# Group-norm centring moved from a matmul into the value weights and first states, with a separate order and PSUM bank for every piece of every group

## Chip, cores and metric

One core of a Trainium2 chip runs the whole program. The metric is the device time of one execution in microseconds (us); lower is better. The time before is 1021.75 us, the median of 3 runs (1021.67 to 1021.78). About 0.2% of that (2 us) is what a measurement can tell from no change.

## What is computed

Two blocks in a row on 64 batches of 64 positions with 256 channels. L0 is a cross attention (16 heads of 16 channels, 128 keys, of which some are masked), an output projection, an rms norm, an MLP with gelu, and a residual. L1 is a recurrent block of the RWKV kind. Cut to what the change touches:

```python
xm = xa[:, :, None] + sx[:, :, None] * (maa_stack + xxx)      # five mixes, low rank xxx
w = exp(-exp(time_decay + tanh(xw @ td_w1) @ td_w2))           # decay; td_w1 is 256 x 64
r, k, v = xr @ Wr.T, xk @ Wk.T, xv @ Wv.T                      # 32 heads of 8 channels
g = silu(xg @ Wg.T)
s0 = state[:, 2:2 + 8].reshape(b, h, 8, 8)                     # the first state of each head
# per position: out_j = sum_i r_i * (u_i * k_i * v_j + s_ij);  s_ij = k_i * v_j + w_i * s_ij
og = out.reshape(b, l, h, 8)
m = og.mean(-1, keepdims=True)
va = ((og - m) ** 2).mean(-1, keepdims=True)
og = ((og - m) / sqrt(va + 1e-05)).reshape(b, l, e) * gn_w + gn_b
x1 = x + og * g @ Wo.T                                         # then a second norm and a feed-forward
```

The output is linear in v_j and in the first state s_ij over j, so the mean over a head's 8 output channels can be taken from the columns of Wv and from the first state instead of from the output.

## The kernel before

**Tiling.** Channels lie on the 128 partitions in two halves. The 64 batches go in 16 groups of 4, so a tile is 128 x 2 x 256 in fp32. Every fp32 matmul shows in the trace as two TensorE instructions (x2 in the counts).

**Pieces.** The work of a group is cut into named pieces, and each engine has a list of `group:piece` tokens that sets its order. There is no scheduler at run time: an engine runs its list and waits on semaphores. Before, a list consists of an explicit start (`PE_FIRST` and so on), one steady turn (`PE_ORDER` and so on) that is repeated for turns 4 to 14, and an explicit end (`PE_LAST`). A steady turn carries the attention of group g+1 together with the recurrent block of group g and the feed-forward of the group before, and so on; in the steady turn every group also uses the same PSUM banks (`BANK`), with exceptions for the first and last groups.

**TensorE pieces used below** (line numbers of the kernel before): `tr0` to `tr7` transposes of attention weights (L528), `sc0`/`sc1` scores (L514), `va0`/`va1` weighted values (L540), `w0` to `w3` and `c0` to `c3` the MLP (L457 and L566), `mean0`/`var0` the first norm of L1 and `mean1`/`var1` the second (all L462), `maa` the low-rank input (L584 full width, then L587 for the fifth mix on 32-column tiles), `xp` and `x4` its outputs (L596, L606), `td1`/`td2` the decay's low rank (L613, L622), `K V R G` (L457), `coef` the bonus weights (L642), `ga0`/`ga1` the sum over i of r_i s_ij on 32-column tiles (L636), `cen` the centring (L646: one 128x128 matrix times 128x512), `gvar` the variance per head (L649), `O`, `fk`, `fr`, `fv` (L457).

**The chain from var0 to xp.** TensorE `var0`; ScalarE `lnr0` (L672, L674); VectorE `nm0` (L957); ScalarE `sh0` (L771); VectorE `sx0` (L969) and `z` (L847); TensorE `maa`; ScalarE `th` (L777, L778); TensorE `xp`. VectorE `tm0` to `tm4` and GpSimd `xm0` to `xm4` (L1063) follow, and then `td1`, K, V, R, G.

**The chain of the recurrence.** ScalarE copies V (`vr`), eight DMAs spread it over partitions, VectorE forms `kv0` to `kv7` (L1002) and runs eight scans `st0` to `st7` (L1011), GpSimd multiplies each by r (`rs0` to `rs7`, L1080), TensorE gathers four at a time (`ga0`, `ga1`). VectorE `sum` (L1021) adds the bonus; TensorE `cen` subtracts the mean into PSUM; ScalarE `gsq` squares it (L818); TensorE `gvar`; ScalarE `lng` (L672, L674); VectorE `gn` (L1025); ScalarE `gu` (L825); VectorE `og` (L1029); TensorE `O`; VectorE `res` (L1033); then the second norm, `fk`, `fr`, GpSimd `act`, `fv`, `fin` and the store.

**Other things.** `WARM` lists places where TensorE runs matmuls of ones (L467) before a piece; they compute nothing that is used. ScalarE switches between two sets of function tables (L684). The first state enters `kv[..., 0]` by a ScalarE copy, `first` (L801). `bonus` shares its memory with `gt`, the gate's tanh, and `gsq`, `g_rs` with `og`.

Of the kernel before, what the change touches and what calls it, by code (L numbers as in the profile page):

```python
# [163 lines left out]

def turns(first, order, last):

    pieces = tokens(order)
# [998 lines left out]
```

## Time and profile before

| | |
|---|---|
| median of 3 runs | 1021.75 us |
| the profiled execution: span, and its own device time | 1021.2 us span; the page gives no second time, so the sum is made on the span |
| TensorE busy (matmul) | 989.1 us, 97% |
| VectorE, ScalarE, GpSimd busy | 723.5, 756.3, 483.4 us |
| steady turn | 58.86 us |
| TensorE clock | 0.997 of full speed on average |

The span lies 0.55 us under the median, so a saving on the span is taken one to one off the median. TensorE is busy nearly all the time from the first group to the last. The steady turn can be read off the chain that ended last, where the same rows come back every 58.86 us ten times, and the last 100 us are different: there TensorE waits for the other engines, and matmuls of ones stand in the gaps.

### The profile page before, as it was taken

What the parts mean: (1) busy time and instruction counts of PE and PEld (TensorE: products, weight loads), DVE (VectorE), ACT (ScalarE), POOL (GpSimd) and SP (SyncE); (2) the same over time, 40 slices, a digit from 0 to 9 for tenths busy, and PEclk for the clock granted to TensorE, in tenths of its full rate; (3) what the DMA queues carried; (4) which work ended last, traced back from release to release, by engine and by line L of the source; (5) the groups of instructions that cost most, each with busy time, mean ns of one, the idle gap of its engine ahead of it and who ended that gap; (6) DMA issues with size and microseconds to landing.
All of it is one profiled execution on the core that took longest, in us unless ns stands there. A gap on an engine that the chain in (4) does not pass through costs nothing.

```text
span 1021.2 us, 19227 instructions
## 1 busy us (share of the span) xinstructions
PE 989.1 (97%) x6914; PEld 740.5 (73%) x6914; DVE 723.5 (71%) x1275; ACT 756.3 (74%) x2034; POOL 483.4 (47%) x391
## 2 busy tenths in 40 slices
...
DMA packets 37662, 60.95 MB, mean 60 GB/s; under 512 B 10496, under 2 KB 13888, under 8 KB 37440
## 3 DMA queue, kind: packets, MB, share of 16 engines
...
q14 instruction: 38, 0.31, 0.1%
...
## 4 chain that ended last, share of the span: by engine, by line
PE 88%; ACT 5%; DVE 4%; issue 2%; POOL 1%; DMA 0%; POOLq 0%; SPq 0%; DVEq 0%; ACTq 0%
PE psum L457 37%; PE psum L566 10%; PE psum L483 6%; PE psum L490 6%; PE psum L528 5%; PE psum L462 3%; PE psum L514 3%; PE psum L540 3%; PE psum L636 3%; PE psum L596 2%; PE psum L646 2%; PE psum L584 1%; PE psum L649 1%; ACT probs L712 1%; PE psum L642 1%
## 5 line engine op out<-in xcount | busy, mean ns | idle before, releaser
L1080 POOL TENSOR_TENSOR rs<-st,rr 128x512 f32<-128x512 f32 x128 | 188.8, 1485 | 232.9 <-DVE st L1011 228.3
L1055 POOL TENSOR_TENSOR probs<-probs,rsum 128x512 f32<-128x512 f32 x128 | 145.3, 1137 | 177.8 <-DVE rsum L900 177.0
L712 ACT ACTIVATE probs<-psum,neg_max 128x128 f32<-128x128 f32 x512 | 180.6, 396 | 17.3 <-DVE neg_max L895 16.9
L684 ACT ACT_TABLE_LOAD x129 | 165.5, 1283 | 2.2
L1011 DVE TENSOR_TENSOR_SCAN st<-decay,kv 128x512 f32<-128x512 f32 x128 | 162.6, 1280 | 1.3 <-POOL rs L1080 1.1
L457 PE MATMUL psum<-xm,w_sb 128*128 128x256 f32 x512 | 122.4, 386 | 0.3
L712 ACT ACTIVATION_READ_ACCUMULATOR probs<-psum,neg_max 128x1 f32 x512 | 120.9, 236 | 0.0
L457 PE MATMUL psum<-y,w_sb 128*128 128x256 f32 x512 | 115.5, 382 | 0.4 <-ACT probs L712 0.3
L457 PEld LDWEIGHTS psum<-xm,w_sb 128*128 128x128 f32 x512 | 95.2, 191 | 27.2 <-issue 12.0
L566 PE MATMUL psum<-hid,w_sb 128*128 128x256 f32 x512 | 114.3, 380 | 0.2 <-ACT hid L741 0.2
L1063 POOL TENSOR_TENSOR xm<-tmp,xs 128x512 f32<-128x512 f32 x80 | 93.6, 1188 | 31.8 <-DVE tmp L989 29.5
L457 PEld LDWEIGHTS psum<-y,w_sb 128*128 128x128 f32 x512 | 96.1, 190 | 16.6 <-issue 3.0
L566 PEld LDWEIGHTS psum<-hid,w_sb 128*128 128x128 f32 x512 | 97.0, 190 | 14.9 <-issue 1.0
L1002 DVE TENSOR_TENSOR kv<-vb,kk 128x504 f32<-128x504 f32 x128 | 101.9, 818 | 0.0
L895 DVE TENSOR_REDUCE neg_max<-psum 128x4 f32<-128x512 f32 x128 | 83.8, 675 | 23.2 <-PE psum L518 23.1
L989 DVE SCALAR_TENSOR_TENSOR tmp<-psum,vec,sx 128x256 f32<-128x256 f32 x128 | 54.5, 477 | 41.1 <-PE psum L596 33.0
L741 ACT ACTIVATE hid<-psum,vec 128x256 f32<-128x256 f32 x128 | 52.2, 472 | 41.0 <-PE psum L566 36.9
L528 PE MATMUL psum<-mats,probs 128*128 128x128 f32 x512 | 69.5, 275 | 1.9 <-ACT r_rs L672 0.7
L528 PEld LDWEIGHTS psum<-mats,probs 128*128 128x128 f32 x512 | 58.2, 141 | 15.6 <-issue 8.2
L905 DVE COPY probs_t<-psum 128x512 f32<-128x512 f32 x64 | 42.7, 685 | 32.2 <-PE psum L528 31.1
L483 PE MATMUL psum<-h_sb,w_sb 128*128 128x512 f32 x128 | 62.9, 616 | 1.0 <-DVE tmp L989 1.0
L457 PE MATMUL psum<-xf,w_sb 128*128 128x256 f32 x256 | 60.4, 381 | 1.8 <-DVE xf L847 1.7
...
## 6 DMA issues: line engine op xcount, KB each, us to landing
vb<-vr SPq DMA_DIRECT2D x128, 256.0 KB, 7.5
...
```

The lines of the kernel that those rows point to most:

```text
L457: last = mm(to[:, n * T:(n + 1) * T], w(name, k, m * P, m * P + P), rhs[k], start=(k == 0), stop=(k == 1))
L483: last = mm(to, w("k", k, m * P, m * P + P), h_sb[:, k, :, :], start=(k == 0), stop=(k == 1))
L528: last = nc.tensor.transpose(to[:, n * P:(n + 1) * P], probs[:, u % PROBS, n, :], mat("ident"))
L566: last = mm(to[:, m * T:(m + 1) * T], w2_sb[:, 2 * n + i, m * P:(m + 1) * P], hid[:, n % 2, i, :], start=(n == 0 and i == 0 and m == 0), s ...
L684: sc.preload_act_table_set(table)
L712: last = fn(probs[:, u % PROBS, n, :], bank(g, f"s{u}")[:, n * P:(n + 1) * P], ACT.Exp, bias=neg_max[:, u % PROBS, n:n + 1], accum_out=sum ...
L895: nc.vector.tensor_reduce(neg_max[:, u % PROBS, :], bank(g, f"s{u}").rearrange("p (n k) -> p n k", n=4), AX.X, ALU.max, negate=True).then_ ...
L1002: tt(kv[:, j, :, 1:S], batches(vb[:, j, :])[:, :, 0:S - 1], batches(flat(kk))[:, :, 0:S - 1], ALU.mult).then_inc(kv_made.sem, 1)
L1011: nc.vector.tensor_tensor_scan(st[:, n % 2, :], decay[:, :, :, :].rearrange("p h b s -> p (h b s)"), kv[:, j, :, :].rearrange("p b s -> p ...
L1055: tt(probs[:, u % PROBS, :, :], probs[:, u % PROBS, :, :], rsum[:, u % PROBS, :].unsqueeze(2).broadcast_to([P, 4, KEYS]), ALU.mult).then_i ...
L1063: tt(xm[:, k % XM, :, :].rearrange("p h (b s) -> p (h b) s", b=GB), tmp[:, k % TMP, :, :].rearrange("p h (b s) -> p (h b) s", b=GB), xs[0] ...
L1080: tt(rs[:, (RH * g + n) % RS, :], st[:, n % 2, :], flat(rr), ALU.mult).then_inc(rs_made.sem, 1)
```

## The change

- **Centring.** The TensorE piece `cen` and its matrix are gone. At the start VectorE takes from each column of Wv the mean over its head (`fold2`: two reductions, four scalar_tensor_tensor). For every group the first state is centred by VectorE (`first` moves there from ScalarE: one reduction to 128x8 and one scalar_tensor_tensor of 128x64). `gsq` and `gn` read the centred sum in SBUF (`bonus`, now a tensor of its own) instead of the PSUM bank of `cen`.
- **32-column tiles.** `td1` is issued as 8 matmuls of 32 weight columns instead of 4 of 64. `maa` is split into the tokens `maaa` and `maab`, which stand next to each other everywhere.
- **Orders and banks.** All five lists are written out for all 16 groups, with no repeated turn, and `BANKS` gives each opened bank by its position. `WARM` goes from 154 matmuls of ones to 138. The lists are some 150 lines of tokens; a line or two tells nothing, so the places on which the prediction rests are shown as instruction orders below.

```diff
-FILLS, FOLDS = 3, 26
+FILLS, FOLDS = 3, 30
...
-def turns(first, order, last):
-
-    pieces = tokens(order)
-    steady = [(i - lag, piece) for i in range(FIRST_TURNS, LAST_TURN) for lag, piece in pieces
-              if 0 <= i - lag < GROUPS and (piece not in ONCE or i == lag)]
-    return tokens(first) + steady + tokens(last)
...
-            bank = GROUP_BANK.get(g, {}).get(name, BANK[name])
+            bank = int(BANKS[len(use)])
...
+        bonus = sb("bonus", [P, HALVES, T])
+        rk, gsq, g_rs = z, og, og
...
                         for i in range(2):
-                            last = mm(to[DD * i:DD * i + DD, 0:TH], w("td1", k), xm[:, (MIX * g) % XM, k, i * TH:(i + 1) * TH], start=(k == 0), stop=(k == 1))
+                            for d in range(2):
+                                at = DD * i + 32 * d
+                                last = mm(to[at:at + 32, 0:TH], w("td1", k, 32 * d, 32 * d + 32), xm[:, (MIX * g) % XM, k, i * TH:(i + 1) * TH],
+                                          start=(k == 0), stop=(k == 1))
...
-                elif piece == "cen":
-                    taken(pe, g, "red")
-                    mm(opened(g, "cen"), center[:, :], flat(bonus), start=True, stop=True).then_inc(filled_by(g, "cen"), 1)
...
-                elif piece == "first":
-                    wait(sc, st_made, g, 0)
-                    wait(sc, s0_in, g, 16)
-                    fn(kv[:, :, :, 0], s0_sb[:, :, :, :].rearrange("p j h b -> p j (h b)"), ACT.Copy).then_inc(first_made.sem, 1)
...
-                    ready(sc, g, "cen")
-                    fn(flat(gsq), bank(g, "cen"), ACT.Square).then_inc(gsq_made.sem, 1)
+                    taken(sc, g, "red")
+                    fn(flat(gsq), flat(bonus), ACT.Square).then_inc(gsq_made.sem, 1)
...
+                    for k in range(2):
+                        nc.vector.tensor_reduce(wv_mean[:, k, :, :], vb[:, k, 0:C].rearrange("p (m j h) -> p m h j", m=HALVES, j=RH), AX.X,
+                                                ALU.add).then_inc(folded.sem, 1)
...
+                elif piece == "first":
+                    wait(ve, st_made, g, 0)
+                    wait(ve, s0_in, g, 16)
+                    flat_s0 = s0_sb[:, :, :, :].rearrange("p j h b -> p j (h b)")
+                    nc.vector.tensor_reduce(s0_mean[:, :], flat_s0.rearrange("p j c -> p c j"), AX.X, ALU.add).then_inc(s0_summed.sem, 1)
+                    wait(ve, s0_summed, g, 1)
+                    stt(kv[:, :, :, 0], s0_mean[:, :].unsqueeze(1).broadcast_to([P, RH, HALVES * GB]), -1.0 / RH, flat_s0,
+                        ALU.mult, ALU.add).then_inc(first_made.sem, 1)
...
-                    wait(ve, gsq_made, g, 1)
+                    taken(ve, g, "red")
                     wait(ve, grstd_made, g, 1)
-                    tt(flat(og), bank(g, "cen"), flat(g_rs), ALU.mult).then_inc(freed_by(g, "cen"), 1)
+                    tt(flat(og), flat(bonus), flat(g_rs), ALU.mult).then_inc(gn_made.sem, 1)
```

TensorE, a steady turn before, from `var0` of one group to the scores of the next. The rows are var0, fr, ga1, fv, tr0 and tr1, maa (two), cen, xp, gvar:

```order
L462 MATMUL psum<-hsum,mats 128x256
L457 MATMUL psum<-xf,w_sb 128x256 x4
L636 MATMUL psum<-rs,heads 32x512 x4
L457 MATMUL psum<-xc,w_sb 128x256 x4
L528 MATMUL psum<-mats,probs 128x128 x8
L584 MATMUL psum<-z,w_sb 128x256 x2
L587 MATMUL psum<-z,w_sb 32x128 x4
L646 MATMUL psum<-gt,center 128x512
L596 MATMUL psum<-th,maa_sb 128x256 x8
L649 MATMUL psum<-og,same 128x512
```

The same place after, in the turn of group 5 (var0, ga1, fr, fv, maaa, maab, tr1 and tr0, xp, gvar):

```order
L514 MATMUL psum<-hsum,mats 128x256
L693 MATMUL psum<-rs,heads 32x512 x4
L509 MATMUL psum<-xf,w_sb 128x256 x4
L509 MATMUL psum<-xc,w_sb 128x256 x4
L636 MATMUL psum<-z,w_sb 128x256 x2
L641 MATMUL psum<-z,w_sb 32x128 x4
L580 MATMUL psum<-mats,probs 128x128 x8
L650 MATMUL psum<-th,maa_sb 128x256 x8
L703 MATMUL psum<-og,same 128x512
```

The two transposes that stood ahead of `maa` now stand behind it, where `cen` was.

ScalarE, near the end before: from the copy of V of group 15 (`vr`). The row `og<-psum` of L818 is `gsq` of group 14, and `rr`, `kk` are R and K of group 15:

```order
L678 ACTIVATE vr<-psum 128x512
L782 ACTIVATE tw<-psum 128x128
L684 ACT_TABLE_LOAD
L787 ACTIVATE decay<-psum,vec 128x4x63 x2
L801 ACTIVATE kv<-s_sb 128x64
L818 ACTIVATE og<-psum 128x512
L793 ACTIVATE decay<-decay 128x8x63
L678 ACTIVATE rr<-psum 128x512
L678 ACTIVATE kk<-psum 128x512
L672 ACTIVATE og<-psum,vec 128x512
```

And after, where `gsq` is L868:

```order
L868 ACTIVATE og<-bonus 128x512
L836 ACTIVATE tw<-psum 128x128
L732 ACTIVATE vr<-psum 128x512
L738 ACT_TABLE_LOAD
L726 ACTIVATE og<-psum,vec 128x512
L728 ACTIVATE og<-og 128x512
L875 ACTIVATE og<-og,gnv 128x256 x2
L732 ACTIVATE kk<-psum 128x512
L786 ACTIVATE decay<-psum,vec 128x4x63 x2
L732 ACTIVATE rr<-psum 128x512
```

The squaring of group 14 has moved from behind group 15's V, tw and e1 to ahead of them.

VectorE, the scans of group 15 before: from the first scan (`st0`), with `kv0` to `kv2` and `og` of group 14 ahead of it:

```order
L1002 TENSOR_TENSOR kv<-vb,kk 128x8x63 x3
L1029 TENSOR_TENSOR og<-og,gate 128x512
L1011 SCALAR_TENSOR_TENSOR st<-decay,kv 128x512
L1002 TENSOR_TENSOR kv<-vb,kk 128x8x63
L1033 TENSOR_TENSOR x<-psum,x 128x512
L940 TENSOR_TENSOR hsum<-x 128x256
L1011 SCALAR_TENSOR_TENSOR st<-decay,kv 128x512
```

And after:

```order
L1095 TENSOR_TENSOR og<-og,gate 128x512
L1099 TENSOR_TENSOR x<-psum,x 128x512
L998 TENSOR_TENSOR hsum<-x 128x256
L1060 TENSOR_TENSOR kv<-vb,kk 128x8x63
L1069 SCALAR_TENSOR_TENSOR st<-decay,kv 128x512
L1060 TENSOR_TENSOR kv<-vb,kk 128x8x63
L1006 TENSOR_TENSOR xc<-x,psum 128x512
L1069 SCALAR_TENSOR_TENSOR st<-decay,kv 128x512
```

`og`, `res` and `hm1` of group 14 now stand ahead of group 15's scans and no longer between them.

## Rows read from the trace of the kernel before

**Rows 1.** Windows: length, then busy us of PE, PEld, DVE, ACT, POOL; clock, DMA

```profile
334.78:393.64 58.86, 58.62 (x423) 45.38 (x423) 43.78 (x79) 46.99 (x128) 30.04 (x25) 1.00 0.33 58
...
805.78:867.71 61.93, 61.04 (x432) 46.38 (x431) 45.28 (x80) 47.73 (x135) 31.04 (x25) 1.00 0.31 52
...
972.00:1021.20 49.20, 36.94 (x162) 19.80 (x162) 23.78 (x32) 14.13 (x23) 13.68 (x10) 1.00 0.03 11
```

**Rows 2.** TensorE timeline, steady turn: start us, length us, line, output and inputs, count

```profile
347.46 0.59 PE L462 MATMUL psum<-hsum,mats 128*128 128x256 f32 x2
347.90 1.89 PE L457 MATMUL psum<-xf,w_sb 128*128 128x256 f32 x8
349.72 1.06 PE L636 MATMUL psum<-rs,heads 128*32 128x512 f32 x8
350.71 1.99 PE L457 MATMUL psum<-xc,w_sb 128*128 128x256 f32 x8
352.54 1.04 PE L528 MATMUL psum<-mats,probs 128*128 128x128 f32 x8
353.42 1.03 PE L584 MATMUL psum<-z,w_sb 128*128 128x256 f32 x4
354.38 0.63 PE L587 MATMUL psum<-z,w_sb 128*32 128x128 f32 x8
354.94 1.12 PE L646 MATMUL psum<-gt,center 128*128 128x512 f32 x2
355.99 1.15 PE L596 MATMUL psum<-th,maa_sb 32*128 32x256 f32 x16
```

**Rows 3.** TensorE timeline, same turn: two 128x512 matmuls, and the next piece

```profile
381.28 1.88 PE L483 MATMUL psum<-h_sb,w_sb 128*128 128x512 f32 x4
383.00 0.59 PE L462 MATMUL psum<-ysum,mats 128*128 128x256 f32 x2
```

**Rows 4.** TensorE timeline, same turn: td1, scores after an idle time, va1

```profile
360.29 0.66 PE L613 MATMUL psum<-xm,w_sb 128*64 128x128 f32 x8
...
361.82 1.17 PE L514 MATMUL psum<-kt,qt 32*128 32x128 f32 x32 [0.24 <-issue]
...
374.57 1.08 PE L540 MATMUL psum<-probs_t,vv 128*32 128x128 f32 x32
```

**Rows 5.** VectorE timeline, steady turn: sx0 and z of the chain to maa

```profile
350.99 1.20 DVE L969 TENSOR_TENSOR sx<-xs 128x512 f32<-128x512 f32 x1 [1.15 <-ACT xs L771]
352.22 0.88 DVE L847 SCALAR_TENSOR_TENSOR z<-sx,vec,xs 128x256 f32<-128x256 f32 x2
```

**Rows 6.** GpSimd timeline, the same moment

```profile
350.61 1.03 POOL L1055 TENSOR_TENSOR probs<-probs,rsum 128x512 f32<-128x512 f32 x1
```

**Rows 7.** TensorE timeline, group 1: its var0

```profile
113.63 0.59 PE L462 MATMUL psum<-hsum,mats 128*128 128x256 f32 x2
```

**Rows 8.** VectorE timeline, group 1: its sx0 and z

```profile
117.23 0.69 DVE L969 TENSOR_TENSOR sx<-xs 128x512 f32<-128x512 f32 x1 [1.15 <-ACT xs L771]
117.96 0.88 DVE L847 SCALAR_TENSOR_TENSOR z<-sx,vec,xs 128x256 f32<-128x256 f32 x2
```

**Rows 9.** VectorE timeline, group 14: its nm0

```profile
883.28 1.48 DVE L957 TENSOR_TENSOR xc<-xc,r_rs 128x512 f32<-128x512 f32 x1 [0.42 <-ACT r_rs L674]
```

**Rows 10.** ScalarE timeline, late: gsq of group 14, Ln of group 15

```profile
956.33 0.60 ACT L818 ACTIVATE og<-psum 128x512 f32<-128x512 f32 x1 [2.80 <-PE psum L646]
...
995.09 0.69 ACT L672 ACTIVATE og<-psum,vec 128x512 f32<-128x512 f32 x1 [0.69 <-PE psum L649]
```

**Rows 11.** VectorE timeline, late: st0 of group 15, then res of group 14

```profile
962.74 1.21 DVE L1011 TENSOR_TENSOR_SCAN st<-decay,kv 128x512 f32<-128x512 f32 x1
...
966.68 0.69 DVE L1033 TENSOR_TENSOR x<-psum,x 128x512 f32<-128x512 f32 x1 [2.16 <-PE psum L457]
```

**Rows 12.** TensorE timeline, late: maa of group 14, ga1 of group 15

```profile
887.67 1.13 PE L584 MATMUL psum<-z,w_sb 128*128 128x256 f32 x4 [0.76 <-DVE z L847]
...
989.39 1.07 PE L636 MATMUL psum<-rs,heads 128*32 128x512 f32 x8 [1.40 <-POOL rs L1080]
```

More of the change, by code:

```diff
@@ L91 @@
-0:x4 1:va1 0:td2 1:o 2:q 0:G 0:coef 1:rms 2:sc0 1:w0 1:w1 1:w2 1:c0 1:c1 1:w3 1:c2 0:ga0 1:c3 2:v0 2:v1 1:mean0 0:ga1 2:tr1 0:cen 1:var0 2:tr2 3:k0
-0:gvar 2:sc1 2:tr0 1:maa 1:xp 3:k1 0:O 2:tr3 1:V 1:K 1:td1 2:va0 0:mean1 2:tr6 2:tr4 2:tr7 2:tr5 1:R 2:va1 1:x4 0:var1 1:td2 2:o 3:q 1:G 2:rms 3:sc0
-3:v0 2:w0 2:w1 2:c0 2:w2 2:w3 2:c1 2:c2 2:c3 1:ga0 2:mean0"""
-PE_ORDER = """3:coef 4:fk 2:var0 4:fr 3:ga1 4:fv 1:tr0 1:tr1 2:maa 3:cen 2:xp 3:gvar 1:v1 1:tr3 2:td1 2:x4 1:sc1 2:V 2:K 1:tr2 3:O 2:R 1:va0 1:tr5 1:tr6 1:tr4 1:tr7
@@ new lines @@
+PE_ORDER = """0:q 0:k0 0:k1 0:sc0 0:v0 0:v1 0:sc1 0:tr0 0:tr1 0:tr2 0:tr3 1:k0 0:va0 1:q 0:tr4 0:tr5 0:tr6 0:bias 0:tr7 1:k1 0:va1 1:sc0 0:o 1:v0 0:rms 1:v1 0:w0
+0:w1 0:w2 0:w3 0:c0 0:c1 0:c2 0:c3 1:sc1 0:mean0 1:tr0 0:var0 1:tr1 1:tr3 1:tr2 2:k0 0:maaa 0:maab 0:xp 2:k1 1:tr5 1:va0 0:td1 0:K 0:V 1:tr4 1:tr6
+1:tr7 0:R 1:va1 0:td2 0:x4 1:o 2:q 0:G 1:rms 2:sc0 0:coef 1:w1 1:w0 1:w2 1:w3 1:c0 1:c1 1:c2 1:c3 0:ga0 2:v0 1:mean0 2:v1 2:tr0 0:ga1 1:var0 2:tr1
+2:sc1 0:gvar 3:k0 2:tr2 1:maaa 1:maab 1:xp 3:k1 2:tr3 0:O 1:K 1:V 1:td1 2:va0 2:tr5 2:tr4 2:tr6 2:tr7 0:mean1 1:R 2:va1 1:td2 1:x4 2:o 3:q 1:G 2:rms
@@ new lines @@
+3:sc0 0:var1 3:v0 2:w0 2:w2 2:w3 2:w1 2:c0 2:c1 2:c2 2:c3 1:ga0 2:mean0 0:fk 1:coef 2:var0 0:fr 1:ga1 0:fv 2:maaa 2:maab 3:tr0 3:tr1 2:xp 1:gvar 3:v1
+2:td1 2:x4 3:sc1 3:tr2 2:V 2:K 3:tr3 1:O 3:va0 3:tr4 3:tr5 2:R 3:tr6 3:tr7 1:mean1 2:td2 3:va1 4:k0 1:var1 3:o 4:q 4:k1 3:rms 4:v0 4:sc0 3:w2 3:w3
+3:w0 3:w1 3:c0 3:c1 2:ga0 3:c2 3:c3 2:G 3:mean0 2:coef 1:fk 3:var0 2:ga1 1:fr 1:fv 3:maaa 3:maab 4:tr1 4:tr0 3:xp 2:gvar 4:v1 3:td1 4:sc1 3:x4 3:V 3:K
+4:tr2 4:tr3 3:R 2:O 4:tr5 4:tr6 4:va0 4:tr4 4:tr7 2:mean1 3:td2 4:va1 5:k0 4:o 5:q 5:k1 4:rms 2:var1 5:v0 5:sc0 4:w2 4:w3 4:w0 4:w1 4:c0 4:c1 4:c2
@@ new lines @@
+4:c3 3:G 3:ga0 4:mean0 3:coef 2:fk 4:var0 2:fr 3:ga1 2:fv 4:maaa 4:maab 5:tr1 5:tr0 4:xp 3:gvar 5:v1 4:td1 5:sc1 4:x4 4:V 4:K 5:tr2 5:tr3 4:R 5:tr4
+3:O 5:va0 5:tr5 5:tr6 5:tr7 3:mean1 4:td2 5:va1 6:k0 5:o 6:q 6:k1 5:rms 6:v0 6:sc0 3:var1 5:w0 5:w2 5:w3 5:w1 5:c0 5:c1 5:c2 5:c3 4:ga0 4:G 5:mean0
+4:coef 3:fk 5:var0 4:ga1 3:fr 3:fv 5:maaa 5:maab 6:tr1 6:tr0 5:xp 4:gvar 6:v1 5:td1 5:x4 6:sc1 6:tr2 6:tr3 5:K 5:R 6:va0 4:O 6:tr4 6:tr5 5:V 6:tr6
+6:tr7 4:mean1 5:td2 6:va1 7:k0 6:o 4:var1 7:q 7:k1 6:rms 7:v0 7:sc0 6:w0 6:w2 6:w3 6:w1 6:c0 6:c1 6:c2 6:c3 5:G 5:ga0 6:mean0 4:fk 5:coef 6:var0 4:fr
@@ new lines @@
+5:ga1 4:fv 6:maaa 6:maab 7:tr1 7:tr0 6:xp 5:gvar 7:v1 6:td1 7:sc1 6:x4 6:V 6:K 7:tr2 5:O 7:tr3 6:R 7:tr4 7:va0 7:tr5 7:tr6 7:tr7 5:mean1 6:td2 7:va1
+8:k0 7:o 8:q 8:k1 5:var1 7:rms 8:v0 8:sc0 7:w3 7:w0 7:w2 7:w1 7:c0 7:c1 7:c2 7:c3 6:ga0 6:G 7:mean0 5:fk 6:coef 7:var0 5:fr 6:ga1 5:fv 7:maaa 7:maab
+8:tr0 8:tr1 7:xp 6:gvar 8:v1 7:td1 7:x4 8:sc1 8:tr3 7:V 7:K 8:tr2 6:O 7:R 8:tr4 8:va0 8:tr6 8:tr5 8:tr7 6:mean1 7:td2 8:va1 9:k0 8:o 6:var1 9:q 9:k1
+8:rms 9:v0 9:sc0 8:w0 8:w3 8:w1 8:w2 7:ga0 8:c0 8:c1 8:c2 8:c3 7:G 8:mean0 7:coef 6:fk 8:var0 7:ga1 6:fr 6:fv 9:tr1 9:tr0 8:maaa 8:maab 7:gvar 8:xp
```

240 lines of the change are left out of this document (159 added, 81 removed), and 28 rows, old and new, of tables (BANK, GROUP_BANK, OPENS).

## Prediction, made before the changed kernel ran

> **What bounds the kernel now.** I read the windows first, one per turn. In the steady turn TensorE is busy 58.62 of 58.86 us, VectorE 43.78, ScalarE 46.99, GpSimd 30.04 [rows 1]. So a steady turn is TensorE's list and nothing else: what leaves that list leaves the time, and the others have 12 us or more of slack a turn. The turn from 805.78 on, the first whose order isn't the repeated one, has 0.89 us without TensorE work (61.93 less 61.04) against 0.24 in a steady turn, and the last 49.20 us have 12.3, with many of the busy ones being matmuls of ones [rows 1]. There the chains through the other engines set the end. Then the TensorE timeline of one turn gives a price for each piece (start to next start), and the timelines of the other engines show how close the chains come to it.
>
> **What leaves TensorE.** `cen` occupies its place for 1.05 us, 354.94 to 355.99 [rows 2]. Two instructions of the plain shape cost half of 1.72 (383.00 less 381.28, four of them), so 0.86 [rows 3]. The other 0.19 is what a change between full and tiled shapes costs on its two sides, since `maab` and `xp` beside it are tiled. After, tr1 and tr0 stand there and pay that 0.19, so I take 0.86 per group and not 1.05. 14 of the 16 `cen` lie where TensorE is the bound (groups 0 to 13): 14 x 0.86 = **-12.0**, at the outside 14 x 1.05 = 14.7. The orders change between full and tiled shapes 250 times in place of 260; 10 x 0.1 = **-1.0**.
>
> **td1.** Before, 8 instructions on two column positions are recorded with 0.66 us; `va1`, 32 instructions of the same length on four positions of 32 columns, with 1.08 [rows 4]. After, td1 is 16 instructions on four positions. Streamed four at a time they take as long as 8 two at a time. I take 0; bounds from these rows are half of 1.08 (-0.1) and, if nothing overlapped more than before, 0.66 more. Times 16 that is -1.9 to +10.6, and the upper end I hold unlikely, since `va1` shows the overlap with just this shape. Splitting `maa` into two tokens that stand together costs nothing.
>
> **Banks.** In each steady turn TensorE idles 0.24 us ahead of sc1 [rows 4]. It has the sc1 banks 3, 0, 6, 4, and bank 0 was x3's, which VectorE frees late. After, each turn has its own banks. I give half of 11 turns: **-1.3** (bounds 0 and -2.6).
>
> **VectorE and ScalarE.** `first` moves to VectorE as two small instructions. Even at the price of a full 128x512 one each, 0.69 [rows 8], that is 1.4 us in a turn that leaves VectorE 15 us [rows 1]; `bonus` as its own tensor only removes a wait. The folding at the start adds four small instructions on net ahead of group 0's `maa`; estimated at 1.5 us by the same row, beside TensorE's MLP of group 0, so 0. Without cover it would be +1.5. ScalarE's order has 103 table loads in place of 129: more slack, no term. `gn` and `gsq` now read SBUF. What they wait for is listed under the rivals.
>
> **The end.** (a) `G` of group 14 (a projection of 8 instructions, 1.7) now comes after group 15's MLP, between its mean0 and var0, where TensorE waits anyway: **-1.7**. (b) Before, gsq of group 14 holds ScalarE idle for 2.80 us until `cen` has filled its bank [rows 10]; decay, R and K of group 15 are queued behind it, and the scans of group 15 behind K. After, gsq stands ahead of group 15's V and needs only `sum`. **-2.8**, bounds 0 and -4. (c) Before, `res` of group 14 stands between the scans of group 15, idle 2.16 and 0.69 long [rows 11]; now it is ahead of them, while K and the spread of V are on their way. The scans run from 962.74 [rows 11] and end in ga1 at 989.39 [rows 12] with VectorE the one that is late, so **-2.9**, bounds 0 and -4. (d) Of the last group, from ga1 at 989.39 [rows 12] to the Ln of lng at 995.09 [rows 10] the chain goes sum, cen, gsq, gvar; without cen -1.05, and gvar no longer stands behind cen and fv together, -0.5: **-1.5**.
>
> **What comes in its place.** The chain var0 to maa. Before, maa starts 5.96 us after var0 (353.42 less 347.46) [rows 2], and z ends at 353.10 [rows 5], so z needs 5.64. After, between var0 and maaa TensorE has only var0 0.44, fr 1.82, ga1 0.99, fv 1.83 = 5.08 [rows 2], since tr0 and tr1 went behind maab. In the groups 2 to 7, 9, 10 and 14, nine turns, the order says this. What z needs at least is seen in group 1: var0 at 113.63 [rows 7], z over at 118.84 [rows 8], 5.21. What it needs at worst so far, group 14: nm0 took 1.48 [rows 9] and TensorE waited 0.76 before maa [rows 12]. So between 0.13 and 0.9 per turn, and as the steady turn lies between (0.56), 9 x 0.5 = **+4.5**, bounds 1.2 and 8. Second, no turn is repeated any more. An order that isn't repeated had 0.65 us more idle per turn (0.89 less 0.24) [rows 1]. 11 turns x 0.4 = **+4.4**, bounds 0 and 7.
>
> **Sum.** -12.0 - 1.0 - 1.3 - 1.7 - 2.8 - 2.9 - 1.5 + 4.5 + 4.4 = -14.3. Against the span of 1021.2 that makes 1006.9, against the median of 1021.75 it is 1007.5.
>
> **Rivals.**
> *The plan holds.* Chains are hidden, stalls of single orders don't come: z 1.2, stalls 0, banks -2.6. -12.0 - 1.0 - 2.6 - 1.7 - 7.2 + 1.2 = -23.3, **998.5**. For it: the tr pair behind maab covers th in full, and ScalarE has fewer table loads in its chains. Against: 5.08 is under the least z has needed.
>
> *VectorE and GpSimd block each other.* In the steady turn sx0 took 1.20 us while a GpSimd pass ran from 350.61 to 351.64 [rows 5, 6], against 0.69 in group 1 with the same operands [rows 8]; nm0 took 1.48 in group 14 [rows 9]. After, the GpSimd order has two or three attention passes in a row where nm0, sx0 and z run, and gn now reads two SBUF tensors while the xm passes run, where it read PSUM before. z at 8, stalls at 7, half of (b) and (c), no banks: -12.0 - 1.0 - 1.7 - 2.9 - 1.5 + 15 = -4.1, **1017.5**.
> By the Trainium skill, page "SBUF — State Buffer", section "Terms", the port pair that VectorE and GpSimd share is exclusive and held for a full instruction, so that the loser blocks. The trace agrees for nm0 and sx0. By that rule each of nm0, sx0 and the halves of z could lose the rest of a pass, and the price is the one given above.
>
> *Slower: the scans come too late.* Groups 5 and 6 have st0 behind five or six kv and their e1, decay behind sh1. From y's normalising to the scan st3 I add up some 15 us of VectorE work, and rs3 on GpSimd ends about 16.1 after it, where TensorE comes to ga0 after w, c and G at about 16.8 (sum of prices of pieces of these kinds; an estimate). The margin is 0.7. If blocking costs VectorE more than 0.7 in that stretch, ga0 stands and everything behind it; at 3 us in 9 turns, 27 less the 19 that is gained otherwise, **1029**. Against: VectorE has 15 us of slack in the turn as a whole [rows 1].
>
> *No change.* TensorE is not what the trace shows as bound, or td1 costs its upper end of 10.6: about **1019 to 1021**. Against it speaks the 58.62 of 58.86.
>
> **Numbers.** Forecast 1007.5, own range 1001 to 1013.5: chance 0.50. The plan holds, 994 to 1001: 0.20. Blocking, 1013.5 to 1019: 0.20. Slower: 0.06. No change: 0.04. The range 995 to 1018 leaves out the last two and the outer edges of the two before. Faster by over 0.2% (2 us, what a measurement of this kernel can tell from none) 0.90, same 0.04, slower 0.06.
>
> **What would show it.** The steady turn after should be near 58.0 plus the waits; 57.5 or less speaks for the plan, 58.5 for blocking. The row of maaa (L636 after) should show idle time released by z (VectorE L897) in nine turns. td1 (L669 after) should keep a place of about 0.6 us. sc1's idle time should be gone in some turns. ScalarE's gsq should no longer wait 2.8 us in the last turns, and ga1 of group 15 should stand about 28 us ahead of the end in place of 31.8 less (d). Wrong would be made the forecast by idle time before ga0 or ga1 in the middle turns, by a turn length that varies by over 1 us, or by a TensorE turn that isn't shorter although cen is gone.

## Result and the profile after

The changed kernel takes 1134.22 us, the median of 4 runs (1133.54 to 1135.54), against 1021.71 us before. The ratio is 1.110, 95% interval 1.107 to 1.112. It is 11% slower, where I forecast 1007.5 us and 0.9 for faster. The page of the kernel after, busy time of each engine and the granted clock in 40 slices:

```profile
span 1131.6 us, 19430 instructions
PE 1003.7 (89%) x6994; PEld 747.6 (66%) x6994; DVE 834.4 (74%) x1311; ACT 720.4 (64%) x1992; POOL 505.5 (45%) x391
PEclk9899999989989899898999989899999999998989
```
```profile
PE 22%; DVE 20%; issue 7%; ACT 4%; POOL 4%; DVEq 0%; POOLq 0%; ACTq 0%
```

The last fence is the chain that ended last, by engine: of what is listed there (57% of the span) TensorE and VectorE have about as much each, where the same view of the kernel before has 88% for TensorE. So TensorE's list doesn't bound the kernel alone any more. Three windows of the middle and one of the end (columns as in [rows 1]):

```profile
370.96:438.13 67.17, 60.57 (x429) 46.22 (x428) 49.58 (x81) 48.61 (x135) 28.15 (x22) 0.95 0.30 52
438.13:505.67 67.54, 60.91 (x429) 47.03 (x428) 51.60 (x81) 44.24 (x122) 32.31 (x25) 0.95 0.29 51
903.55:966.79 63.24, 59.46 (x430) 45.32 (x429) 47.42 (x78) 43.12 (x125) 27.92 (x21) 0.97 0.31 53
1082.00:1131.60 49.60, 37.40 (x154) 20.68 (x152) 27.95 (x33) 13.69 (x21) 16.55 (x12) 0.93 0.05 14
```

A turn takes 59.6 to 70.5 us from the third on, where [rows 1] had 58.86 with 58.62 busy. Of the two first windows TensorE leaves over 6 us idle. Taken from the start of c0 in each group: the head is 12.0 us longer (group 0's c0 at 58.26 in place of 46.23), the fifteen turns together 95.4, the stretch behind the last c0 3.0 (103.8 less 100.8). That makes up the 110.4 us between the spans.

What TensorE waits for after, in total, times, longest:

```profile
PE psum L514 <- DVE hsum L998: 52.2, 16, 6.5
PE psum L636 <- DVE z L897: 16.8, 12, 3.1
PE psum L693 <- POOL rs L1146: 9.4, 10, 2.1
PE psum L535 <- DMA h_sb<-hT: 9.1, 1, 9.1
PE psum L509 <- POOL xm L1129: 7.6, 3, 3.7
```

L514 behind hsum is `mean0`, L636 is `maaa`, L693 `ga0` and `ga1`. Before, the list of waits began at 2.8. 69.0 of these 95.1 us are waits for VectorE. Two pieces of group 5's turn: TensorE behind its wait for hm0, with the window of the last row (columns as in [rows 1], the clock third from the end), then VectorE and GpSimd:

```profile
385.61 1.22 PE L514 MATMUL psum<-hsum,mats 128*128 128x256 f32 x2 [4.66 <-DVE hsum L998]
386.62 1.91 PE L699 MATMUL psum<-z,bonus_w 128*128 128x256 f32 x4
388.33 2.92 PE L509 MATMUL psum<-xf,w_sb 128*128 128x256 f32 x8
```
```profile
388.33:391.25 2.92, 2.92 (x10) 2.41 (x9) 1.93 (x6) 1.25 (x1) 0.00 (x0) 0.64 0.00 0
```
```profile
394.61 1.20 DVE L1027 TENSOR_TENSOR sx<-xs 128x512 f32<-128x512 f32 x1
395.85 2.32 DVE L897 SCALAR_TENSOR_TENSOR z<-sx,vec,xs 128x256 f32<-128x256 f32 x2
```
```profile
394.23 4.84 POOL L1121 TENSOR_TENSOR probs<-probs,rsum 128x512 f32<-128x512 f32 x4
```

A projection of 8 instructions (fk here) takes 2.92 us behind 4.66 us of idle time, where one of the same shape takes 1.89 in [rows 2] (fr). The granted clock is 0.50 from 385.61 to 388.33, the lower of TensorE's two levels (1.2 GHz, against 2.4), and 0.64 on average over the projection. And z takes 2.32 us for its two halves (0.88 in the turn of experiment 1 at 350.79), while four attention passes run on GpSimd in a row, as the change's list has them.

The costliest groups of VectorE (busy, mean ns, idle before):

```profile
L1069 DVE TENSOR_TENSOR_SCAN st<-decay,kv 128x512 f32<-128x512 f32 x128 | 196.8, 1554 | 14.1 <-POOL rs L1146 13.4 <-ACT decay L847 0.3
L897 DVE SCALAR_TENSOR_TENSOR xf<-sx,vec,xs 128x256 f32<-128x256 f32 x64 | 46.3, 767 | 0.4
L897 DVE SCALAR_TENSOR_TENSOR z<-sx,vec,xs 128x256 f32<-128x256 f32 x32 | 24.3, 799 | 0.9
```

Before, the scan's mean was 1280 ns (162.6 us busy), xf's 515 and z's 481. One interval shows the difference: from the end of y's normalising (yn) to the start of x1 on VectorE. Before it is 14.4 us in each of the turns 3 to 12, with less than 0.1 us of idle time in it. After it is 18.6 to 22.8 in the groups 3 to 14, with one exception of 14.7. x1 and hm0 feed mean0. The interval is a symptom and not the length of the turn, as experiments 3, 10 and 13 show.

### The profile page after: what moved, and what is told of

The parts are those of the page before. It is cut to its first block, busy times and chain, and to the rows that moved or that the text cites. A ratio compares the mean times of both kernels' runs of the same rounds, so it can differ in the third digit from the quotient of the medians.

```text
span 1131.6 us, 19430 instructions
## 1 busy us (share of the span) xinstructions
PE 1003.7 (89%) x6994; PEld 747.6 (66%) x6994; DVE 834.4 (74%) x1311; ACT 720.4 (64%) x1992; POOL 505.5 (45%) x391
## 4 chain that ended last, share of the span: by engine, by line
PE 22%; DVE 20%; issue 7%; ACT 4%; POOL 4%; DVEq 0%; POOLq 0%; ACTq 0%
PE psum L509 9%; DVE st L1069 6%; DVE kv L1060 3%; PE psum L580 2%; POOL rs L1146 2%; DVE neg_max L952 2%; PE psum L535 2%; DVE sx L1027 2%; DVE xf L897 1%; PE psum L514 1%; PE psum L592 1%; POOL xm L1129 1%; DVE xc L1015 1%; PE psum L650 1%; PE psum L636 1%
## 5 line engine op out<-in xcount | busy, mean ns | idle before, releaser
L1146 POOL TENSOR_TENSOR rs<-st,rr 128x512 f32<-128x512 f32 x128 | 200.5, 1576 | 329.2 <-DVE st L1069 289.2
L1069 DVE TENSOR_TENSOR_SCAN st<-decay,kv 128x512 f32<-128x512 f32 x128 | 196.8, 1554 | 14.1 <-POOL rs L1146 13.4
L1121 POOL TENSOR_TENSOR probs<-probs,rsum 128x512 f32<-128x512 f32 x128 | 141.3, 1117 | 116.8 <-DVE rsum L957 116.3
L509 PE MATMUL psum<-xm,w_sb 128*128 128x256 f32 x512 | 126.5, 396 | 8.3 <-POOL xm L1129 7.6
L1129 POOL TENSOR_TENSOR xm<-tmp,xs 128x512 f32<-128x512 f32 x80 | 100.9, 1280 | 65.8 <-DVE tmp L1047 42.1
L509 PEld LDWEIGHTS psum<-xm,w_sb 128*128 128x128 f32 x512 | 98.6, 198 | 27.7 <-POOL xm L1129 12.0
L1060 DVE TENSOR_TENSOR kv<-vb,kk 128x504 f32<-128x504 f32 x128 | 107.1, 866 | 2.6 <-ACT kk L732 2.6
L514 PE MATMUL psum<-hsum,mats 128*128 128x256 f32 x128 | 46.5, 449 | 53.9 <-DVE hsum L998 52.2
L795 ACT ACTIVATE hid<-psum,vec 128x256 f32<-128x256 f32 x128 | 53.0, 471 | 51.6 <-PE psum L618 37.0
L803 ACT ACTIVATE sq<-xc 128x512 f32<-128x512 f32 x32 | 20.2, 632 | 95.0 <-DVE xc L1006 95.0
L509 PE MATMUL psum<-xf,w_sb 128*128 128x256 f32 x256 | 70.8, 427 | 5.6 <-DVE xf L897 5.6
L535 PE MATMUL psum<-h_sb,w_sb 128*128 128x512 f32 x128 | 63.3, 620 | 10.2 <-DMA h_sb<-hT 9.1
## 6 DMA issues: line engine op xcount, KB each, us to landing
w_sb<-W SPq DMA_DIRECT2D x1, 1024.0 KB, 10.7
```

Source lines behind the costliest of these rows:

```text
L509: last = mm(to[:, n * T:(n + 1) * T], w(name, k, m * P, m * P + P), rhs[k], start=(k == 0), stop=(k == 1))
L535: last = mm(to, w("k", k, m * P, m * P + P), h_sb[:, k, :, :], start=(k == 0), stop=(k == 1))
L1060: tt(kv[:, j, :, 1:S], batches(vb[:, j, :])[:, :, 0:S - 1], batches(flat(kk))[:, :, 0:S - 1], ALU.mult).then_inc(kv_made.sem, 1)
L1069: nc.vector.tensor_tensor_scan(st[:, n % 2, :], decay[:, :, :, :].rearrange("p h b s -> p (h b s)"), kv[:, j, :, :].rearrange("p b s -> p ...
L1121: tt(probs[:, u % PROBS, :, :], probs[:, u % PROBS, :, :], rsum[:, u % PROBS, :].unsqueeze(2).broadcast_to([P, 4, KEYS]), ALU.mult).then_i ...
L1129: tt(xm[:, k % XM, :, :].rearrange("p h (b s) -> p (h b) s", b=GB), tmp[:, k % TMP, :, :].rearrange("p h (b s) -> p (h b) s", b=GB), xs[0] ...
```

## Experiments

Thirteen kernels ran. My first theory (A): the new orders bring the scans late, so that more of them stand between yn and x1. Rivals: (B) the centring itself costs on VectorE, (C) td1's tiles cost, (D) the head is a matter of one DMA, (E) the clock is what makes waits expensive, (P) VectorE and GpSimd block each other.

**1. The computation without the orders.** All of the changed computation, but lists, banks and repeated turns of the kernel before. The cut is shortened and shows the kind of edit.

```diff
-PE_ORDER = """0:q 0:k0 0:k1 0:sc0 0:v0 0:v1 0:sc1 ...        (each group its own)
+PE_FIRST, PE_ORDER, PE_LAST, BANK, GROUP_BANK of the kernel before, without cen
-ACT: ... 2:first ...
+DVE: ... 4:fin 2:first 2:tm0 ...
```

> The computation of the changed kernel (centring in Wv and first states, td1 on 32-column tiles) in the order, banks and repeated turns of the kernel before; only cen falls out and first goes to VectorE's list ahead of tm0. Theory A (the orders cost the time, by scans that come too late): turn near 58.0, no wait of mean0 for hsum, total 1005 to 1012. Theory B (centring on VectorE and the SBUF-reading gn and gsq cost it): slower than 1060, with mean0 waiting for hsum in the steady turn. Theory C (td1's 32-column tiles cost it): td1's place grows by 0.6 us or more, total 1017 to 1030.

1015.56 us, ratio 0.994 (0.992 to 0.996). So the centring and td1 gain 6 us, and **the orders, with their banks and their unrepeated turns, cost 118.7**. Of the 7.8 us between the spans (1013.4 for 1021.2) 4.8 lie behind the last c0 and 2.9 in the fifteen turns. B is gone: with the same instructions VectorE is busy 738.7 us here, 834.4 in the changed kernel. Theory A's number, though, was too good. Its turn is 58.70 us in place of 58.86, only 0.16 less, though TensorE lost 1.05 us of work. The rows tell why (the TensorE timeline of this kernel, and its waits):

```profile
352.94 0.63 PE L590 MATMUL psum<-z,w_sb 128*32 128x128 f32 x8
354.21 1.15 PE L599 MATMUL psum<-th,maa_sb 32*128 32x256 f32 x16 [0.64 <-ACT th L781]
...
360.23 1.17 PE L515 MATMUL psum<-kt,qt 32*128 32x128 f32 x32 [0.44 <-DVE tmp L996]
```
```profile
PE psum L599 <- ACT th L781: 9.7, 15, 0.7
PE psum L515 <- DVE tmp L996: 4.6, 11, 0.4
```

`cen` had stood between maa and xp and covered ScalarE's tanh; without it xp waits 0.64 for th. sc1 behind it waits 0.44 where it waited 0.24 [rows 4], now for VectorE's tmp. 1.05 less 0.64 less 0.20 leaves 0.2. TensorE's list was full, but a piece on it was also the cover of a chain.

**2. td1 alone.** The kernel before with td1 on 32-column tiles.

```diff
-last = mm(to[DD * i:DD * i + DD, 0:TH], w("td1", k), ...)
+for d in range(2):
+    at = DD * i + 32 * d
+    last = mm(to[at:at + 32, 0:TH], w("td1", k, 32 * d, 32 * d + 32), ...)
```

> The kernel before with td1 alone on 32-column tiles. My working: 0, so 1021.7 within 1. If the 16 instructions don't overlap four at a time, +10.6: 1032.

1022.65 us, ratio 1.000 (0.999 to 1.001), and a turn of 58.86. C is gone, and the 0 of my sum stands.

**3. Scans early.** The changed kernel, two lists mended in groups 3 to 12.

```diff
 ACT  ... g+1:ev1
+     g:K g:R g:e1 g:decay
      g+1:ysq ...                  (they stood behind qt, kt, lna)
 DVE
+     g:first g:kv0 g:kv1 g:st0
      g+1:y g+1:ysum
+     g:st1 g:kv2
      g+1:yn
+     g:st2 g:kv3
```

> The changed kernel with two lists altered for the groups 3 to 12: on ScalarE K, R, e1 and decay stand ahead of the next group's ysq, on VectorE first, kv0, kv1 and st0 stand ahead of the next y, st1 behind ysum, st2 behind yn. Theory A: ten turns lose their mean0 waits (3.3 us each) and what the clock loses behind them (about 2), so 1134 less 30 to 60: 1075 to 1105. Theories B and C: no difference over 5 us.

1120.99 us (1114.58 to 1125.21), 13 less, and not the 30 to 60 of theory A. mean0 waits 28.4 us in place of 52.2, but a new wait stands beside it: the mean of ysum (the rms norm), 10.2 us in 9 times, since y now stands behind scans that wait for decay. From yn to x1 the groups 4 to 13 are 30.5 us shorter together, and less than half of that comes back in the total. So late first scans alone don't explain the changed kernel.

**4. h of group 1 ahead of load1** on SyncE.

```diff
-0:load0 1:mask 0:load1 0:s0 0:xa 1:h
+0:load0 1:mask 1:h 0:load1 0:s0 0:xa
```

> The changed kernel with SyncE issuing h of group 1 ahead of load1. If the head's 12 us come from h queued behind the weights, k0 of group 1 doesn't wait 9.1 us any more and the total falls by 8 to 12, to 1122 to 1126. If the weights then come late for w0 and maaa instead, it falls by less than 4.

1123.22 us, 11.0 less. D holds for the head. SyncE, then TensorE in the changed kernel:

```profile
14.84 4.51 SPq L487 DMA_DIRECT2D w_sb<-W  x2
...
21.23 1.05 SPq L443 DMA_DIRECT2D h_sb<-hT  x1
30.93 3.78 PE L535 MATMUL psum<-h_sb,w_sb 128*128 128x512 f32 x4 [9.11 <-DMA h_sb<-hT]
```

The same issues of SyncE in the kernel before, h and the two loads of reordered weights:

```profile
17.84 0.33 SPq L391 DMA_DIRECT2D h_sb<-hT  x1
...
24.75 1.23 SPq L435 DMA_DIRECT2D w_sb<-W  x2
```

h (512 KB) is issued 3.4 us later than before, at 21.23 for 17.84, behind the weights of load1. It lands 9.7 us after its issue, before 3.8 (4.6 in this experiment), and TensorE waits 9.11 for it. The two loads of reordered weights ahead of it take 4.51 us to issue. That isn't their own cost: before, and in this experiment, the same two take 1.23. From 14.84 to 21.23 the DMA engines of the changed kernel are busy all the time, at 373 GB/s. With h issued earlier group 0's c0 starts at 48.15 and not at 58.26.

**5. and 6. Short rs passes, with the new and with the old order.** Both leave most of the readout out: rs is made on 32 of 512 columns only.

```diff
-tt(rs[:, (RH * g + n) % RS, :], st[:, n % 2, :], flat(rr), ALU.mult)
+tt(rs[:, (RH * g + n) % RS, 0:32], st[:, n % 2, 0:32], flat(rr)[:, 0:32], ALU.mult)
```

> The changed kernel with each of GpSimd's 128 rs passes on 32 of its 512 columns (the other columns of rs stay zero, so the readout is wrong; rs on TensorE keeps its size). VectorE is busy 95.7 us longer in the changed kernel than with the same computation in the old order (834.4 against 738.7). Theory P (the scans stand back to back and meet the rs passes on the port that the two engines share): VectorE's busy time falls to 760 or less, the scan to 1.2 to 1.3 us, the total by 50 or more, under 1085. Theory O (only the length of VectorE's list ahead of hm0 counts, not the meeting with GpSimd): the total falls by less than 20.

> The same computation in the old order, with each rs pass on 32 of 512 columns (readout wrong in the same way). TensorE bounds that kernel, so both theories expect 1008 to 1016, with VectorE's busy time down by 20 to 40 from 738.7.

1028.26 us and 1010.92 us, the first as theory P expects, the second as both theories do. The four spans:

| span, us | rs on 512 columns | rs on 32 | difference |
|---|---|---|---|
| old order, same computation | 1013.4 | 1009.2 | 4.2 |
| new order | 1131.6 | 1026.3 | 105.3 |
| difference | 118.2 | 17.1 | |

Of the 17.1 left with short passes 10.7 are the head (c0 of group 0 at 57.34 against 46.63). So in everything behind the head the new order is 6.4 us worse by itself, and some 100 us come only when the rs passes have their full length. The banks and the unrepeated turns are the same in both rows of the new order, so by themselves they too cost no more than these 6.4. VectorE and GpSimd of the new order with short passes, and kv of the changed kernel beside them:

```profile
L1069 DVE TENSOR_TENSOR_SCAN st<-decay,kv 128x512 f32<-128x512 f32 x128 | 159.6, 1263 | 1.8 <-ACT decay L847 0.3 <-issue 0.3
L1060 DVE TENSOR_TENSOR kv<-vb,kk 128x504 f32<-128x504 f32 x128 | 88.0, 717 | 2.6 <-ACT kk L732 2.6
L1147 POOL TENSOR_TENSOR rs<-st,rr 128x32 f32<-128x32 f32 x128 | 79.1, 621 | 344.1 <-DVE st L1069 287.8 <-PE psum L693 43.0 <-ACT rr L732 12.2
```
```profile
L1060 DVE TENSOR_TENSOR kv<-vb,kk 128x504 f32<-128x504 f32 x128 | 107.1, 866 | 2.6 <-ACT kk L732 2.6
```

The scan is back at 1263 ns, VectorE's busy time falls by 90.9 to 743.5, its waits for rs (13.4) are gone, and the stretch from yn to x1 is 14.3 to 18.0. Of the 90.9 us the scans have 37.2, kv 19.1 and xf 15.6. With the old order VectorE's busy time falls by 28.3 too, and the kernel gains only 4.2. Theory P: yes, as far as VectorE's busy time goes. But a short rs also shortens the chain scan, rs, scan after next (st has two buffers), and GpSimd's own list (505.5 us busy, 381.8 with short passes), and this pair doesn't part them. Run 13 asks whether passes outside that chain cost anything.

**7. and 8. Late scans in the old order.** The reverse of 3: the old order with moves of the kind that the new lists make (decay and the first scans behind y's norm). Run 7 has both lines, run 8 the second alone.

```diff
-ACT_ORDER: 1:ev1 2:decay 3:lnr1 1:ysq 0:qt 0:kt1 0:kt0 1:lna 0:vv0
+ACT_ORDER: 1:ev1 3:lnr1 1:ysq 0:qt 0:kt1 0:kt0 1:lna 2:decay 0:vv0
-DVE_ORDER: 2:ysum 4:nm1 3:kv2 3:st1 2:yn 3:st2 ... 2:kv1 1:fold0 2:st0 1:y
+DVE_ORDER: 2:ysum 4:nm1 3:kv2 2:yn 3:st0 3:st1 3:st2 ... 2:kv1 1:fold0 1:y
```

> The same computation in the old order, with two moves in the repeated turns that the changed kernel's lists also have: decay on ScalarE behind ysq, qt, kt and lna, and st0 on VectorE behind yn. If late scans are what makes mean0 wait: 11 turns with 1 to 3 us each, 1027 to 1049. If the old order has slack enough for it: 1014 to 1019, and what costs the changed kernel is more than the scans' start.

> The computation of the changed kernel in the old order, with one move of the two in late_scans: st0 on VectorE behind yn, decay in its old place. One more scan (1.2 us) in the stretch from yn to x1. If each microsecond in that stretch is one of the turn: 11 turns x 1.2 to 2.3, 1029 to 1041. If the stretch has slack: 1014 to 1018, and decay was the costly part of late_scans (67 us).

1082.89 and 1085.77 us: 67 and 70 more than experiment 1. **Moving two scans (st0, and st1 with it) behind yn costs about 6 us a turn** (64.43 for 58.70 in the trace of run 8), and decay's place nothing that these runs tell. Both expectations were far too low. VectorE in run 8, one turn:

```profile
468.16 0.69 DVE L935 TENSOR_TENSOR y<-y,a_rs 128x512 f32<-128x512 f32 x1 [2.40 <-ACT a_rs L677]
468.77 2.33 DVE L1018 TENSOR_TENSOR_SCAN st<-decay,kv 128x512 f32<-128x512 f32 x2
472.20 2.27 DVE L1018 TENSOR_TENSOR_SCAN st<-decay,kv 128x512 f32<-128x512 f32 x1 [1.09 <-POOL rs L1095]
474.39 1.26 DVE L901 TENSOR_REDUCE neg_max<-psum 128x4 f32<-128x512 f32 x2
```
```profile
470.07 2.10 POOL rs L1095
...
472.20 0.04 DVE st L1018
...
472.34 2.05 issue
474.39 0.67 DVE neg_max L901
...
475.08 1.51 ACT probs L715 x8
...
476.64 5.41 PE psum L458 x16
```

TensorE at the same place, w0 and w1, then w2 and w3:

```profile
469.15 3.72 PE L458 MATMUL psum<-y,w_sb 128*128 128x256 f32 x16
476.64 5.41 PE L458 MATMUL psum<-y,w_sb 128*128 128x256 f32 x16 [3.77 <-ACT probs L715]
```

The second fence is the chain through the same microseconds. Three scans in a row: beside the second the first rs pass takes 2.10 us (1.27 where it is alone), the third scan waits 1.09 for it (two buffers) and then takes 2.27 itself, beside the second rs pass. The attention maxima mx0 and mx1 are queued behind it, at 474.39, 5.54 us behind yn's end; in experiment 1 they begin 1.06 behind it. ScalarE's exp waits for them, and TensorE's w2 for the bank that the exp frees: 39.9 us in 12 times. Two scans of 1.2 us ahead of a queue turned into 4.5. Behind the wait w2 and w3 take 5.41 us at a granted clock of 0.68, where w0 and w1 with as many instructions take 3.72. So of the 5.73 us a turn 3.77 are the wait and 1.69 the lower clock behind it. This is not what the changed kernel waits for: in most of its turns mx0 stands ahead of the first scan behind yn, and it waits at mean0. The pair shows the price of such a move, not that the changed kernel pays it at this place.

**9. Ones ahead of mean0.** The changed kernel keeps TensorE busy in its longest wait.

```diff
-WARM = {..., (0, "q"): 11}
+WARM = {..., (0, "q"): 11, (3, "mean0"): 12, ... (14, "mean0"): 12}
```

> The changed kernel with 12 matmuls of ones (some 2.6 us) ahead of mean0 in the groups 3 to 14, where TensorE waits for hsum 3.3 us on average. If the idle time lowers the clock and that costs about 2 us a turn behind it: granted clock from 0.961 to over 0.98 and the total down by 10 to 25, 1110 to 1124. If the lower clock is hidden by VectorE, the late one: within 5 of 1134.

1135.93 us, ratio to before 1.111. The clock rose from 0.961 to 0.971, where I wanted 0.98, and the time did not fall. In group 5 the ones did their work: fk behind mean0 takes 1.89 us again, not 2.92, and then maaa waits 1.89 for z, as it waited 1.90 in the changed kernel. So at this place E is gone: the slow projections behind mean0 are hidden by VectorE, which is late anyway. In run 8, where TensorE is the late one, the lower clock did cost.

**10. and 11. x1 early, and three mends together.**

```diff
 DVE, groups 3 to 14
+     g:x1 g:hm0
      g-1:st5 ...
-     g:x1 g:hm0
```

> The changed kernel with x1 and hm0 moved up on VectorE, ahead of the scan st5 of the group before (in turns where they stood behind it). From the end of y's normalising to x1 it has 18.6 to 22.8 us in the changed kernel, 14.4 in the kernel before. Theory A: that stretch is the loop; with one to three scans (1.3 to 2.3 us each) behind x1 the stretch falls by 2 to 4 and the total by 20 to 40, to 1094 to 1114. Rival: ga1 and rs then stand late by as much, since the scans moved behind x1 feed them, and the total stays within 8 of 1134.

> The changed kernel with three mends together: h of group 1 ahead of load1, decay and the first scans early as in scans_early, x1 and hm0 ahead of st5. If they add up: 1134 - 11 - 13 - (20 to 40) = 1070 to 1090. If blocking between VectorE and GpSimd is spread over the whole turn, so that a mend at one place comes back at the next: over 1100.

1151.32 and 1142.16 us: **slower** than the changed kernel, the first outside both of its expectations, the second on the side of blocking. Here theory A in its narrow form falls: from yn to x1 the groups 3 to 14 together are 38.5 us shorter in run 10 and 51.6 in run 11, and the totals are 17 and 8 us longer. TensorE's waits in run 10:

```profile
PE psum L509 <- DVE xf L897: 37.6, 11, 7.7
PE psum L514 <- DVE hsum L998: 18.1, 10, 5.2
PE psum L514 <- DVE hsum L1011: 16.6, 9, 6.4
```

The wait for hm0 fell from 52.2 to 18.1 us, and the one for xf rose from 5.6 to 37.6, the one for hv0 (L1011) from 1.8 to 16.6. I read this so: not one place of VectorE's list is late but the whole of it from yn to z, and who is moved ahead puts the next one behind.

**12. tr1 as cover.** Experiment 1 with one piece moved on TensorE.

```diff
-4:fv 1:tr0 1:tr1 2:maaa 2:maab 2:xp
+4:fv 1:tr0 2:maaa 2:maab 1:tr1 2:xp
```

> The computation of the changed kernel in the old order, with tr1 in the repeated turns behind maab in place of ahead of maaa. In the old order without cen, xp waits 0.64 us for th in every repeated turn, and z ends 0.32 ahead of maaa. So tr1 (0.52) covers th, and maaa may wait 0.2 for z: 11 x 0.4, so 1009 to 1013. If z is later than the row says, it stays at 1015.

1014.49 us, ratio 0.993 (0.992 to 0.994), the turn 58.54. th's waits fall from 9.7 to 3.8 us. In a turn TensorE's idle time falls from 1.08 to 0.40 us, and the turn by 0.16 only, as the pieces take longer when they alternate: tr0 and tr1 0.60 and 0.66 us apart and 1.04 together, maaa 1.13 in place of 1.03. It is the fastest kernel of the study, 8 us ahead of before, but above the 1009 to 1013 expected and only 1 ahead of experiment 1, within what these runs tell apart.

**13. Short pn passes with the new order.** Leaves most of the attention's normalising out, and keeps scan and rs as they are.

```diff
-tt(probs[:, u % PROBS, :, :], probs[:, u % PROBS, :, :], rsum[...].broadcast_to([P, 4, KEYS]), ALU.mult)
+tt(probs[:, u % PROBS, :, 0:8], probs[:, u % PROBS, :, 0:8], rsum[...].broadcast_to([P, 4, 8]), ALU.mult)
```

> The changed kernel with each of GpSimd's 128 pn passes (the attention probabilities times the inverse sum) on 32 of its 512 columns, so most probabilities stay unscaled and the output is wrong; the rs passes keep their size, and so does the handshake between a scan, its rs and the scan after next. Theory P (every GpSimd pass that meets a VectorE pass on SBUF operands lengthens it): VectorE's busy time falls by 20 or more from 834.4, sx, z, xf and xc most, and the total by 25 or more, to under 1109. Theory H (small_rs_new won its 106 us because the chain scan, rs, scan got shorter, blocking is a side show): the total within 10 of 1134.

1109.92 us, 24.3 less, a hair short of the 25 that theory P wanted and far from theory H's 10. VectorE is busy 27.1 us less (807.3), though none of its instructions changed:

```profile
L897 DVE SCALAR_TENSOR_TENSOR z<-sx,vec,xs 128x256 f32<-128x256 f32 x32 | 15.8, 533 | 0.9
```

z falls from 799 to 533 ns, and maaa's waits from 16.8 to 6.0 us; the scan stays (1534 ns). From yn to x1 nothing changes (0.4 us in twelve groups together). So passes outside the scan's chain cost too, and a chain of scan and rs can't be the reason there. How the 105 us of the rs passes divide between longer VectorE passes (90.9 us of busy time), the chain (VectorE's 13.4 idle, and what ga0 and ga1 wait, 9.4) and GpSimd's shorter list stays open: no run gave st a third buffer, which would part them.

By the Trainium skill, page "SBUF — State Buffer", section "Terms", VectorE and GpSimd share a port pair that one of them holds for a full instruction. These runs agree: a scan of 1.2 us takes 2.27 beside an rs pass, and an rs pass of 1.27 takes 2.10 beside a scan, while mx, which reads PSUM, has a mean of 674 ns after and 675 before.

## Why the prediction was wrong

The step that failed is the one that let VectorE go at nothing: no term of the sum is a wait of TensorE for VectorE's hm0. In its place TensorE waits 52.2 us at mean0 for it, VectorE is busy 834.4 us where the same computation in the old order keeps it busy for 738.7 (experiment 1), and the turns vary from 59.6 to 70.5 us, a sign of being wrong that I had named.

- **The sum's frame.** I priced TensorE's list and let VectorE go as "12 us or more of slack a turn" [rows 1]. Slack of a turn as a whole says nothing of a stretch. From yn to x1 VectorE is busy for 14.4 us without idle time. That interval was there to be read, and I read it only as far as ga0.
- **The rival "the scans come too late"** named a part of the mechanism, at a chance of 0.06 and with a price of 27 us for nine turns. It is shown in the old order (runs 7 and 8); in the changed kernel the first scans brought forward in ten turns gave 13 us back (run 3). Three things in it were off. The place: I counted to st3 and ga0, and the queue's next customers, x1 and hm0 for mean0, are the ones that wait (52.2 us against 9.4). The extent: I saw it in groups 5 and 6, but the lists have seven or eight scans behind ysum in every turn (seven before), and mostly six or seven between yn and x1 (five before). The price: 15 us of work summed at the durations of a well spaced list, where scans in a row meet their own rs passes. Experiment 8 shows 6 us a turn for one such move of two scans; I had said 3.
- **The rival "VectorE and GpSimd block each other"** was priced at 0.9 a turn through z, +15 in all (1017.6 by its own sum, where it says 1017.5). Measured are 1.4 a time for z and maaa (16.8 in 12) and far more through the scans, kv and xf: 105 us hang on the rs passes, 24 on the pn passes. I treated two rivals apart that belong together: late scans are scans without spacing, and those meet their rs passes.
- **z before maaa, +4.5** (bounds 1.2 and 8): 16.8 us of waiting. The mechanism was right. The nine turns of the term have 9.3 of it, over the upper bound, and the other groups 7.5, which the term left out; nm0's 1.48 of [rows 9] was not the worst case: four GpSimd passes in a row now run beside z.
- **cen, 14 x 0.86 = -12.0.** In the old order it brought 0.16 a turn, since xp then waits 0.64 for th and sc1 0.20 more. In the new order tr1 and tr0 cover th, as I said, but nothing is left of the gain.
- **td1, 0:** right, 1.000 (0.999 to 1.001). In experiment 1 td1's 16 instructions are recorded with 0.64 us at 358.51, before the 8 were with 0.66 [rows 4].
- **VectorE and folding, 0:** the two instructions of first are 0.26 and 0.46 us in experiment 1, and its turn is no longer for them. Right as long as VectorE is hidden; in the changed kernel the second of them has a mean of 0.64.
- **The head.** My sum had no term for it, and it costs 11 to 12 us. I had not followed SyncE's list, where h of group 1 had gone behind load1.
- **The end.** (d) holds: from ga1 of the last group to the end it is 30.0 us (1101.58 to 1131.6), 31.8 before, so -1.8 against -1.5. (b) failed: ScalarE now idles 5.68 us ahead of gsq of group 14, released by VectorE's sum, with K and R queued behind it as before. (c) failed in its effect: res stands ahead of the scans, as the list says, and the first of them begins at 1074.18, behind it, hm1 and one kv. From the last c0 to ga1 it is 73.8 us, 69.0 before, so the -7.4 of (a), (b) and (c) turned into +4.7. How much of that is (a), G of group 14, no run parts. ScalarE, then VectorE in the changed kernel:

```profile
1062.89 0.63 ACT L868 ACTIVATE og<-bonus 128x512 f32<-128x512 f32 x1 [5.68 <-DVE bonus L1087]
```
```profile
1072.24 0.69 DVE L1099 TENSOR_TENSOR x<-psum,x 128x512 f32<-128x512 f32 x1 [2.16 <-PE psum L509]
...
1074.18 1.23 DVE L1069 TENSOR_TENSOR_SCAN st<-decay,kv 128x512 f32<-128x512 f32 x1
```

- **Unrepeated orders, +4.4** (0 to 7): with short rs passes, behind the head, the new orders lose 6.4 on the whole, all other terms included. The term was a fair price for the orders alone and none for what they do together with rs passes of full length.
- **Banks, -1.3:** TensorE's waits for nothing that the profile shows ahead of sc1, 2.6 us in 11 times before, are down to 0.2 in one. The term was right at its place, and nothing of it is left in the total. For the -1.0 of fewer changes between full and tiled shapes no run shows a number.
